# Two-layer gated cross-attention on one core: a token tile prepared a stage early, weight transfers reordered, a ternary product split by halves, and a query unit put between two key units

## The reference, cut to what matters

```
x = x + tanh(g_xattn[0]) * xattn0(layernorm(x), ctx, ctx)      # 16 heads of 32
x = x + tanh(g_ffn[0])   * ffn0(layernorm(x))                  # ternary weights, 8-bit activations
x = x + tanh(g_xattn[1]) * xattn1(layernorm(x), ctx, mask)     # 8 heads of 64, masked
x = x + tanh(g_ffn[1])   * ffn1(layernorm(x))                  # four-bit weights and activations

xattn:  q = x @ Wq; k = ctx @ Wk; v = ctx @ Wv; softmax(q k^T * scale) v @ Wo
ffn0:   bit_linear(silu(depthwise_conv3(bit_linear(x, w1))), w2)
        bit_linear: x * 127/max|row| rounded, w / mean|w| rounded to -1, 0, 1
ffn1:   fp4(h) @ fp4(w_down).T,  h = silu(fp4(x) @ fp4(w_gate).T) * (fp4(x) @ fp4(w_up).T)
        fp4: blocks of 16, scale = max|block|/6, values to the grid 0 .5 1 1.5 2 3 4 6
```

## Time and profile before

| | |
|---|---|
| time, median of 3 runs | 2136.84 us (2135.51 to 2139.83) |
| the profiled execution: its own time, and its span | 2135.8 us, 2134.0 us |
| mean granted clock of TensorE over the span, as a share of full | 0.937 |
| busy: PE, PEld | 1846.3 us (87%), 1279.2 us (60%) |
| busy: DVE, ACT, POOL | 1424.4 us (67%), 995.2 us (47%), 1237.6 us (58%) |
| share of the 16 DMA engines that SP's queue took | 38.9% |
| stretches of the blocks, from the span's start | a0 to 711 us, f0 to 1019, a1 to 1767, f1 to 2134 |

### The profile page before, as it was taken

How to read it: one execution, slowest core, us unless ns; L and a number is a source line. 1 busy time by engine, 2 the same in 40 slices (tenths; PEclk the granted TensorE clock), 3 DMA queues, 4 the chain that set the end, 5 groups by cost and what they waited for, 6 DMA issues and landing times. The chain is left out here.

```text
span 2134.0 us, 41071 instructions
## 1 busy us (share of the span) xinstructions
PE 1846.3 (87%) x14610; PEld 1279.2 (60%) x14610; DVE 1424.4 (67%) x2598; ACT 995.2 (47%) x1276; POOL 1237.6 (58%) x1462
## 2 busy tenths in 40 slices
PE   5799999999997469997578999999999975899995
PEld 3467677777776367785346676666666662444442
DVE  4677777776765468885343766766767545889872
ACT  3167667766768596764214443434344341111110
POOL 3166766766766333443202766766667534988963
PEclk9899999999997579998889999999999997999998
DMA  7445445445430501111633443544444381323322
GB/s 204 107 109 134 108 118 134 110 120 133 119 86 24 179 23 53 35 43 35 186 96 84 122 140 112 149 116 141 120 133 142 98 171 45 72 71 82 79 66 67
DMA packets 271226, 222.41 MB, mean 104 GB/s; under 512 B 149976, under 2 KB 239832, under 8 KB 270552
## 3 DMA queue, kind: packets, MB, share of 16 engines
q1 hardware_dynamic: 271064, 220.22, 38.9%
HBM read 129.96 MB, written 67.53 MB: 93 GB/s over the span
## 5 line engine op out<-in xcount | busy, mean ns | idle before, releaser
L716 POOL TENSOR_TENSOR a_p_hl<-a_p,a_p_hl 125x448 bf16<-125x448 f32 x540 | 563.5, 1045 | 467.2 <-ACT a_p_hl L856 432.0
L846 ACT ACTIVATE a_p<-a_psum 125x1344 f32<-125x1344 f32 x192 | 248.0, 1291 | 134.7 <-PE a_psum L1276 127.6
L1025 DVE TENSOR_REDUCE a_nm<-a_psum 112x1 f32<-112x750 f32 x256 | 237.4, 934 | 99.8 <-PE a_psum L1296 99.4
L856 ACT ACTIVATE a_p_hl<-a_p 125x1344 bf16<-125x1344 f32 x192 | 254.3, 1324 | 103.8 <-PE a_psum L1314 100.2
L1314 PEld LDWEIGHTS a_psum<-a_v_st,a_p_hl 125*128 125x128 bf16 x4608 | 179.5, 99 | 40.5 <-issue 19.2
L1314 PE MATMUL a_psum<-a_v_st,a_p_hl 125*128 125x65 bf16 (+2 forms) x4608 | 191.2, 196 | 11.0 <-POOL a_p_hl L716 5.4
L1186 PE MATMUL a_psum<-a_chl,a_w 128*128 128x375 bf16 x768 | 143.4, 333 | 23.2 <-DVE a_w L915 14.4
L1186 PE MATMUL a_psum<-a_chl,kept_w 128*128 128x375 bf16 x768 | 139.3, 335 | 21.5 <-DVE kept_w L915 18.5
L1296 PE MATMUL a_psum<-kept_k,a_q_st 128*112 128x375 bf16 (+1 forms) x512 | 124.3, 343 | 33.8 <-DMA kept_k<-a_k 15.3
L1296 PE MATMUL a_psum<-a_k_st,a_q_st 96*112 96x375 bf16 x512 | 128.9, 338 | 25.6 <-DVE a_nm L1025 18.5
L1186 PE MATMUL a_psum<-a_w,a_chl 128*125 128x512 bf16 x576 | 139.9, 385 | 8.6 <-DVE a_m_parts L1006 5.7
(11 more groups left out here) (237 smaller groups left out, 3856.3 us busy)
## 6 DMA issues: line engine op xcount, KB each, us to landing
a_k<-a_k_tmp SPq DMA_DIRECT2D x64, 375.0 KB, 3.0
a_k_st<-a_k SPq DMA_DIRECT2D x96, 187.5 KB, 3.4
kept_k<-a_k SPq DMA_DIRECT2D x96, 187.5 KB, 3.4
a_c<-in_ctx_t SPq DMA_DIRECT2D x16, 750.0 KB, 5.8
ctx_parts<-a_chl SPq DMA_DIRECT2D x16, 750.0 KB, 9.6
a_chl<-ctx_parts SPq DMA_DIRECT2D x16, 750.0 KB, 6.7
a_q_st<-a_q SPq DMA_DIRECT2D x192, 56.0 KB, 2.2
parts<-a_fhl SPq DMA_DIRECT2D x24, 352.0 KB, 4.0
```

The costliest lines, as they stand in the source:

```text
L716: ins = nc.gpsimd.tensor_tensor(p_hl[0:MC, h % 2, 1, cols], p32[0:MC, h % 2, cols], p_hl[0:MC, h % 2, 0, cols], ALU.subtract)
L846: nc.scalar.activation(p32[0:MC, par, :].rearrange("p (b n) -> p b n", b=3), st[0:MC, :, 0:2 * S], ACT.Exp, scale=scale).then_inc(exp_done, 1)
L856: nc.scalar.activation(p_hl[0:MC, par, 0, :], p32[0:MC, par, :], ACT.Copy).then_inc(phi_done, 1)
L1025: ins = nc.vector.tensor_reduce(out, sm_[0:HALF, 0:2, 0:MK], AX.XY, ALU.max, negate=True)
```

## The change: what it does, and the diff

There are five edits.

1. Tile 0 of f1 is taken through its steps, up to the two bf16 parts, inside a1's last row, in buffers of the weight rounding (`first_x`, `first_n`, `first_t`). SP loads it in quarter 2; DVE does moments (quarter 2), normalising and scaling (quarter 3) and the low part (quarter 0 behind the row); POOL does root and rounding at the end of quarter 2; ACT does the high part at the end of quarter 3; SP turns it with two DMA_TRANSPOSE ahead of the last pair for the weights. f1 then starts with PE on tile 0 and with the steps of tile 1 on the others.
2. In `weight_pieces` the store of a finished piece moves ahead of the query's `regroup` in quarters 0 to 2, and in quarter 0 the load of the next piece moves from the end of quarter 3 behind the mask and residual loads.
3. In f0 the down product goes by halves of channels: q = 0 for both s, then `prepare`, then q = 1 for both s. DVE rounds the two halves of hidden values one place earlier, POOL does its first scaling ahead of the row's root, and ACT rounds the next input ahead of `row_factors`.
4. In a1's quarter 3 the query unit goes between the two key units: K(0,0), Q(0), K(0,1) in place of Q(0), K(0,0), K(0,1).
5. PE's Q(0) waits for the unit two before it, no longer for the one before it.

```diff
@@ quarter_units (a1, quarter 3)
-                units += chunk[2:] + chunk[:2]
+                units += chunk[:1] + chunk[2:] + chunk[1:2]
@@ weight_pieces (SP)
-                last = unit[0] == "K" and unit[1][1] == 1 if q == 3 else unit[0] == "Q"
-                if last and 1 <= m <= FP4_PIECES:
+                if unit[0] == "K" and unit[1][1] == 1 and 1 <= m <= FP4_PIECES:
                     sp.wait_ge(f_split, m)
-                    if m + 1 < FP4_PIECES:
-                        load_weight_piece(m + 1)
                     sp.dma_start(fp4_weights[m - 1][1], fhl[:, :, :]).then_inc(fw_sent, 16)
+                if q == 0:
+                    if unit == ("K", (1, 0), b + 1) and 2 <= m < FP4_PIECES:
+                        sp.wait_ge(f_split, m - 1)
+                        load_weight_piece(m)
+                if unit[0] == "Q" and q != 3 and 1 <= m < FP4_PIECES - 1:
+                    sp.wait_ge(f_split, m)
+                    load_weight_piece(m + 1)
@@ quarter (SP)
+                if q == 2 and b.number == B - 1 and kept:
+                    sp.wait_ge(f_split, FP4_PIECES)
+                    sp.wait_ge(out_sent, 33)
+                    sp.dma_start(first_x, x_out[0, ...][0:P, :]).then_inc(first_in, 16)
+                if q == 0 and b.number == B and kept:
+                    sp.wait_ge(first_low, 1)
+                    for part in range(2):
+                        sp.dma_start(kept.first_input()[:, part, :, :], fhl[:, part, 0:D],
+                                     transpose=True).then_inc(kept.first_turned, 16)
                 if q == 0 and b.number == B and kept:
                     sp.wait_ge(st_ready, B * H + H)
                     kept.load(sp, 1)
@@ first_tile (POOL), called at the end of quarter 2 of the last row
+                pool.wait_ge(first_moments, 1)
...
+                ins.then_inc(first_root, 1)
+                pool.wait_ge(first_scaled, 1)
+                chain.link(nc.gpsimd.tensor_tensor(first_t, first_t, first_x, ALU.add))
+                chain.link(nc.gpsimd.tensor_tensor(first_t, first_t, first_x, ALU.subtract))
+                fp4_rescale(nc.gpsimd, first_n, first_t, ...).then_inc(first_rounded, 1)
@@ quarter (ACT)
+                if kept and q == 3 and b.number == B - 1:
+                    act.wait_ge(first_rounded, 1)
+                    act.wait_ge(fw_sent, FP4_PIECES * 16)
+                    nc.scalar.activation(fhl[:, 0, 0:D], first_n, ACT.Copy).then_inc(first_high, 1)
@@ first_tile (DVE)
+                if at == (2, 0):
+                    dve.wait_ge(first_in, 16)
+                    link(nc.vector.bn_stats(first_stats, first_x))
+                    nc.vector.bn_aggr(first_mv, first_stats).then_inc(first_moments, 1)
+                if at == (3, 0):
+                    dve.wait_ge(first_root, 1)
+                    link(nc.vector.tensor_scalar(first_n, first_x, ...))
+                    fp4_scale(link, first_n, ..., first_x, first_t, 1e-12).then_inc(first_scaled, 1)
+                if at == (0, 0):
+                    dve.wait_ge(first_high, 1)
+                    nc.vector.tensor_tensor(fhl[:, 1, 0:D], first_n, fhl[:, 0, 0:D], ALU.subtract).then_inc(first_low, 1)
@@ unit_products (PE)
-                if (unit[:2] == ("OP", 0) and not (stacked and (b + 2).exists())
-                        or unit[:2] == ("Q", 0) and not stacked and (b.number is None or b.number >= 2)):
+                if unit[:2] == ("OP", 0) and not (stacked and (b + 2).exists()):
@@ bit_ffn, POOL turn: row_roots(b + 1) behind the first of the eight scalings
@@ bit_ffn, ACT turn
                     if g == 6 and in_range(b + 1):
                         scale_input(b + 1)
+                        round_input(b + 1)
                         row_factors(b + 1)
-                    if g == 7 and in_range(b + 1):
-                        round_input(b + 1)
@@ bit_ffn, DVE turn: round_hidden(.., 0) at g == 5 ahead of PREPARE, round_hidden(.., 1) at g == 6
@@ bit_ffn, PE turn
-                    for s in range(2):
-                        if s == 1 and in_range(b + 1):
-                            prepare(b + 1)
-                        for c in range(FC):
+                    for q in range(2):
+                        pe.wait_ge(hq_ready, b * 2 + q + 1)
+                        for s in range(2):
+                            for c in range(q * QH, (q + 1) * QH):
...
+                        if q == 0 and in_range(b + 1):
+                            prepare(b + 1)
@@ fp4_ffn: tile 0 is skipped by SP, POOL, ACT and DVE, PE waits for first_turned; DVE start
             make_h(0, 0, 0)
             x_normalise(2)
             make_h(0, 0, 1)
             x_scale(2)
             make_h(0, 0, 2)
```

More of the change, by code:

```diff
@@ L1146, in quarter @@
                     weight_step(q, b, 2 * j + 1)
+                    if kept and (b.number == B - 1 and q in (2, 3) or b.number == B and q == 0):
+                        first_tile((q, j))
                     for unit in slots[4 * j + 3]:
@@ L1609, in turn @@
             def turn(b, par):
-                if in_range(b + 1) and not (isinstance(b, int) and b == 0):
-                    row_roots(b + 1)
                 if in_range(b - 1):
@@ L1616, in turn @@
                         for n in range(QH // 2):
+                            if q == 0 and n == 1 and in_range(b + 1):
+                                row_roots(b + 1)
                             part = h[:, 1 - par, q * QH + 2 * n:q * QH + 2 * n + 2, :]
@@ L1917, in turn @@
                         add_centre(b, g)
+                    if g == 5 and in_range(b - 1):
+                        round_hidden(b - 1, 1 - par, 0)
                     if g in PREPARE and in_range(b + 1):
                         PREPARE[g](b + 1)
-                    if g in (6, 7) and in_range(b - 1):
-                        round_hidden(b - 1, 1 - par, g - 6)
+                    if g == 6 and in_range(b - 1):
+                        round_hidden(b - 1, 1 - par, 1)
                     if g == 6 and in_range(b):
@@ L2107, with __init__, first_input @@
 class KeptTiles:
-    def __init__(self, w_sb, k_st, parts, landed):
-        self.w_sb, self.k_st, self.parts, self.landed = w_sb, k_st, parts, landed
+    def __init__(self, w_sb, k_st, parts, landed, first_turned):
+        self.w_sb, self.k_st, self.parts, self.landed, self.first_turned = w_sb, k_st, parts, landed, first_turned
+    def first_input(self):
+        flat = self.w_sb[:, 0:3, :, :, :].rearrange("p w t c n -> p (w t c n)")
+        return flat[:, 3 * 2 * KC * D - 2 * KC * P:].rearrange("p (a c s) -> p a c s", a=2, c=KC)
     def tile(self, n):
@@ L2241, in _ @@
             sp.sem_inc(hT_in, 1)
-            for t in (1, 2, 3):
+            for t in (2, 3):
                 sp.wait_ge(xn_ready, t)
@@ L2338, in turn @@
                     x_round(t + 3)
-            for t in range(3):
+            pool.sem_inc(roots, 1)
+            pool.sem_inc(xq_ready, 1)
+            for t in (1, 2):
                 x_root(t)
@@ L2460, in _ @@
             dve.sem_inc(hb_ready, 1)
-            x_moments(0)
-            x_normalise(0)
-            x_scale(0)
+            for done in (moments, xn_ready, x_scaled, xb_ready):
+                dve.sem_inc(done, 1)
             x_moments(1)
-            x_lo(0)
             x_normalise(1)
@@ L2470, in _ @@
             dve.wait_ge(gate_ready, 1)
+            make_h(0, 0, 0)
             x_normalise(2)
+            make_h(0, 0, 1)
             x_scale(2)
-            for g in range(NG):
-                make_h(0, 0, g)
+            make_h(0, 0, 2)
             turns(dve.Fori, turn, lambda i: own.enter_loop(i, 2 * FFN1_LINKS),
@@ L2487, in gate_up @@
                 c0, w = GROUPS[g]
+                turned = kept.first_input() if number_known(t) and t == 0 else xqT[:, par, :, :, :]
                 for n, bank in enumerate((gp, up)):
@@ L2534, in program @@
         k_st = ctx.enter_context(nc.sbuf_tensor("kept_k", [P, 2, 16 * M], BF16))
-        kept = KeptTiles(w_sb, k_st, parts, [nc.alloc_semaphore(f"weights_in{n}") for n in range(3)])
+        kept = KeptTiles(w_sb, k_st, parts, [nc.alloc_semaphore(f"weights_in{n}") for n in range(3)],
+                           nc.alloc_semaphore("first_turned"))
         cross_attention(nc, "a1", x2, x3, ctx_t, ctx_parts, (Wq1, Wkv1[:, 0:D], Wkv1[:, D:2 * D], Wo1), g_xattn[1:2],
```

49 lines of the change are left out of this document (41 added, 8 removed).

## The result

The changed kernel takes 2161.45 us (median of 4 runs, 2157.61 to 2165.72), against 2136.65 us before (4 runs): the ratio is 1.0119, 95% interval 1.0092 to 1.0146, so it is slower by 24.8 us. The profiled execution is the shortest of the four, with a span of 2155.8 us, 21.8 above the span before. Some of the difference between the two figures lies in a0, whose program is the same: f0's first load is issued at 714.40 us, before at 719.34.

A forecast was written before the change was run, and what follows sets the result against it. PE, busy 87%, was taken to bound the kernel. Terms +24.0 + 5.0 - 2 - 13 + 1.8 (tile 0 together) = +15.8 gave 2151.6 us against the profiled execution, 2153 against the median; range 2130 to 2167.

The forecast's parts named there:

- Seam, +24.0: At a1's six seams the query's round trip on SP delays the keys' write by 4.0 us each: +24.0 (20 to 28).
- the clock, +5.0: Behind a1's seams, longer PE waits make matmuls restart at half clock: +5.0 us (+1.2 to +7.2).
- Weight transfers, -2: In a1, the weight load no longer directly behind the keys' reads on SP shortens PE's key waits: -2 us (-4 to 0).
- Ternary, -13: In f0, two PE waits a turn for rounded values go, later maxima take some back: -13 us (-16 to -8).
- Tile 0 in a1, +15.1: At a1's end, tile 0's steps delay head 6's low part, the last weight pair and residual load: +15.1 us (11.1 to 16).
- in f1, -13.3: PE starts f1 at once, the first hidden reduction comes earlier, and the gain stays until the end: -13.3 us (-18.9 at best).
- The first rival: At a1's seams the query's low part ends early enough that SP is free for the keys: 2124 us, chance 0.13.
- the second (the end of a1 does not move): At a1's end, tile 0's parts fit in POOL's idle time, so little is delayed: 2139 us, chance 0.12.
- the third (the ternary order gives nothing): In f0, ACT's earlier rounding delays the maxima so much that no gain is left: 2166 us, chance 0.13.

The follow-up runs named there:

- seam_alone: The kernel before with only the query unit between the key units at the seam and its wait two units back; ratio 1.0156 to before.
- tile_alone: The kernel before with only tile 0 of f1 prepared in a1's last row; ratio 1.0043 to before.
- ternary_alone: The kernel before with only f0's down product by channel halves and its earlier rounding; ratio 0.9935 to before.
- two steps moved: Kernel before plus early tile 0, with POOL's rounding moved behind head 6's low part and SP's transposes behind the residual load; ratio 0.997 to before.
- all steps moved: Same two moves, plus DVE's scaling one head later and ACT's high and DVE's low part behind the turned output; ratio 0.9962 to before.

## Why the prediction was right

The forecast was slower, 2153 us in a range of 2130 to 2167. The sign, the main mechanism and the range held; the size came out 8.5 us low. That it came so near is in part luck: the weights' gain was 7 us larger than forecast and tile 0's cost 7 us larger, and the two cancel. Term by term, each as an edit by itself (ratio times about 2133 us):

- **Seam, +24.0 and the clock, +5.0, together +29.** Measured +33 alone (27 to 39). The waits grew by 3.8 a seam in that kernel, 22.8 in all, and by 4.1 between the changed kernel and the one without these edits; the slower restarts cost 3.6. One term was missing, PE's earlier need of the context, 2.5. Some 4 us of the 33 are in none of these. The path was as forecast. Counted back from PE's arrival at the seam, the keys were written 6.1 us ahead before (6.4 once), and at five seams of the changed kernel they are written 2.5 to 2.7 us ahead. That is 3.4 to 3.9 later, where the forecast had 3.3 to 4.2; at the seam with the landing of 3.62 it is 5.3 later. The changed kernel's wait is 34.8 and not near 40, since edit 2 shortens it. The Trainium skill ("DMA: Bandwidth & Descriptors", section "Anatomy of one DMA — SWDGE (gpsimd) path") gives about 2.0 us as the fixed cost of a transfer that GpSimd issues, a condition that the prediction left out; here SP issues. The landings of 1.87 and 1.88 us are near it. The one of 3.62 is not, nor are two of the six in the trace of before, 2.35 and 4.16.
- **Weight transfers, -2 (-4 to 0).** Mis-sized: -9 measured (-12 to -5). The keys' wait fell by 4.4, and the restarts behind shorter waits were faster by 2.7. The prediction bounded the gain by 1.92, the shorter of the two waits in its rows, and gave it no share of the clock. The trace of before already has one of 1.74, and in the kernel with this edit alone they are 1.45 to 1.73 at five of six seams.
- **Ternary, -13.** Measured -14. The step that ACT's earlier rounding makes the maxima late by 1.0 was right to the tenth (0.98 in the trace). The gain a turn is 1.3 in the profile, not 1.6. Against before, 4.9 us are gained up to f0's last load of a row, 5.8 from there to the first seam, and 3.2 in the five rows of a1 behind it, where the waits and restarts are shorter.
- **Tile 0 in a1, +15.1, and in f1, -13.3.** The order of events was as forecast on each engine. Both sizes were off: +17.7 and -10.5 alone, +9 in all, where +1.8 was predicted (-4 to +3.5). The steps that were priced too low can be read in the changed kernel, where f1 starts 20.0 later. The two transposes took 2.53 us: the prediction used 1.25 for both, which is what one instruction takes in the earlier trace rows. The last pair took 13.26 for 11.10. On POOL rounding took 4.9 (1763.51 to 1768.40) for 3.78, and root 4.7 (from the end of head 4's low part at 1755.03 to DVE's start at 1759.70) for 3.36. These are 5.8 us; behind the residual load 1.3 of them came back. In f1, the first hidden division did come 23.6 us after the start (24.2 forecast), a gain of 14.0, and the later tiles did follow at nearly the old pace: at the last tile's division the gain is still 13.1. What failed is that it "stays until the end": 2.1 us are lost behind that division, where the last two down products took 9.83 and 9.56 us for 8.74 and 9.00.

Added up, the four kernels with one part each give 33 - 9 - 14 + 9 = +19, the change +25 (20 to 31); the sums agree within their intervals. The first rival (the seam does not lengthen) is excluded by `seam_alone`, the second (the end of a1 does not move) by `tile_alone`, the third (the ternary order gives nothing) by `ternary_alone`, though it is what happens when ACT's piece is left out.

## What to carry to other kernels

Before two units change places, write down for the in-order queue that ships their results what each unit makes it do: a unit that becomes ready late drags its whole round trip in front of the next. Where two round trips must follow one another, issue both writes ahead of the first wait. Work moved into an idle stretch needs a free place on every engine that it crosses, and a wait removed on one shows up on the next: 17.7 us of delay here became 6.1 by moving two steps and stayed at 6.1 by moving all.

## What the runs showed of the hardware

A wait at the seam costs more than itself, and by steps. PE in the kernel without the seam's edits, and in the changed kernel, from the restart to the next group of score products:

```profile
1280.54 0.98 PE L1368 MATMUL a_psum<-kept_k,a_q_st 128*112 128x375 bf16 x4 [1.52 <-DMA kept_k<-a_k]
1284.43 0.94 PE L1368 MATMUL a_psum<-kept_k,a_q_st 128*112 128x375 bf16 x4
```

```profile
1291.59 1.68 PE L1367 MATMUL a_psum<-kept_k,a_q_st 128*112 128x375 bf16 x4 [5.23 <-DMA kept_k<-a_k]
1298.26 0.94 PE L1367 MATMUL a_psum<-kept_k,a_q_st 128*112 128x375 bf16 x4
```

The same matmuls take 3.89 us where the granted clock is 1.00 of 2.4 GHz throughout, and 6.67 where they begin at the 1.2 GHz level, with a mean of 0.55. In between lie restarts of some 5.5 us, with a mean of 0.67 to 0.69. In the kernel without the seam's edits three of four waits between 1.52 and 1.60 us were followed by 3.89, one by 5.52; in the one with the weight transfers alone, four of five between 1.45 and 1.73 by some 5.5. Over 3.89 a seam, the six restarts cost 10.8 us before, 3.2 without the seam's edits and 14.4 with them alone. With the weight transfers alone they cost 8.1. That two kernels with nearly the same waits differ by 5 us in this is not explained by any run here.

The late landings at the seams go with a transfer on another queue. Most writes of a query chunk land in 1.87 to 1.89 us there, and most of the keys in some 3. In the thirteen kernels where PE waits for the keys at all six seams, ten query writes took over 3.5 us and seven key writes over 4. In each of these seventeen waits the profile has a packet of the instruction queue, and in most of the shorter ones it has none. In the case shown above the DMA engines had moved all but 17 small packets by 1461.4 and were 2% busy from there to 1463.5, so other traffic on them didn't hold the landing up. This is an association: fourteen other waits with such a packet were of the usual length, and no run varied it.

An instruction of POOL took longer while DVE did its low part of the probabilities (`a_p_hl`, 125x1344). L770 took 2.46 us beside it, and L769, with operands of the same form, 1.26 just ahead of it. In the kernel with two steps moved the same instruction took 2.46 with that work beside it; in the one with all steps moved, without it, 1.27. It is 1.2 of the 5.8 us above.

The same program in a0 took from 712.0 to 721.9 us in the profiled executions, measured to f0's first load. That is why differences under 5 us can't be read from one pair of profiles, and why the terms above are checked on stretches of their own.
